# Key and query stacks made in place in 32-partition bands, with three banded score products per unit

## What is computed

```python
def gnn(h_target, h_neigh, adjacency, Wq, bq, Wk, bk, Wv, bv, Wo, bo, E):
    msg = h_neigh[None, :, :] + E[edge_types]          # edge_types is the adjacency
    q = (h_target @ Wq.T + bq).reshape(Bt, H, DH)      # h_target = layernorm(x)
    k = (msg @ Wk.T + bk).reshape(Bt, Bn, H, DH)
    v = (msg @ Wv.T + bv).reshape(Bt, Bn, H, DH)
    scores = jnp.einsum('bhd,bnhd->bhn', q, k) / np.sqrt(DH)
    scores = jnp.where(adjacency[:, None, :] == 0, -1e9, scores)
    attn = jnp.where(adjacency[:, None, :] == 0, 0.0, softmax(scores))
    return jnp.einsum('bhn,bnhd->bhd', attn, v).reshape(Bt, d) @ Wo.T + bo
x = x + gnn(...)
x = x + ffn(layernorm(x))   # tree: 8 levels, node = 2*node + (score > 0) + 1,
                            # out += gelu(|score|) * (x @ w2s[node] + b2s[node])
```

## Time and profile before

| what | us |
|---|---|
| median of three runs | 159.88 (159.72 to 160.49) |
| the profiled execution's own time | 160.56 |
| its span, first to last instruction | 157.9 |
| setup, to the first scores (L492 starts) | 23.6 |
| units 0 to 7 | 23.6 to 38 |
| units 8 to 31 | 38 to 76 |
| projection, tree walk, sorting | 76 to 107 |
| loop over the nodes | 107 to 158 |

### The profile page before, as it was taken

The page is one execution under the profiler, slowest core; times in us unless marked ns, Lnnn a source line. Parts: engine busy times, 40 slices in busy tenths (PEclk is TensorE's granted clock), DMA queues, the critical chain, the costliest instruction groups (busy, mean ns, idle before and its releaser), DMA issues.

```text
span 157.9 us, 3163 instructions
## 1 busy us (share of the span) xinstructions
PE 105.4 (67%) x870; PEld 78.5 (50%) x871; DVE 109.5 (69%) x302; ACT 73.5 (47%) x174; POOL 40.1 (25%) x82
## 2 busy tenths in 40 slices
...
GB/s 144 293 128 158 173 116 14 57 83 150 393 407 401 457 452 415 399 460 437 311 44 28 0 0 0 53 18 0 0 4 0 0 2 0 0 33 0 0 17 17
DMA packets 6341, 22.35 MB, mean 142 GB/s; under 512 B 1755, under 2 KB 4826, under 8 KB 5722
## 3 DMA queue, kind: packets, MB, share of 16 engines
...
q10 hardware_dynamic: 1104, 0.92, 2.0%
q0 software_dynamic: 256, 0.52, 1.1%
...
...
## 4 chain that ended last, share of the span: by engine, by line
PE 32%; DVE 19%; DMA 14%; issue 13%; ACT 8%; SPq 6%; POOL 3%; DVEq 3%; ACTq 0%; POOLq 0%
PE s_ps L660 10%; DMA early<-q_parts 7%; SPq L249 6%; PE turn_ps L523 4%; PE turn_ps L660 4%; ACT prob L391 4%; DVE prob L770 3%; DMA w_sb<-in_w_t 2%; PE aux_ps L660 2%; ACT prob_t L387 2%; POOL early L337 2%; DMA q_parts<-q_p 2%; PE misc_ps L660 2%; PE s_ps L492 2%; PE s_ps L502 2%
## 5 line engine op out<-in xcount | busy, mean ns | idle before, releaser
L523 PE MATMUL turn_ps<-ident,prob 128*128 128x128 f32 x128 | 23.0, 308 | 7.9 <-ACT prob L391 6.6
L391 ACT ACTIVATE prob<-prob,negmax 128x512 f32<-128x512 f32 x32 | 23.0, 720 | 9.6 <-DVE negmax L770 9.5
L349 POOL TENSOR_TENSOR early<-early,scaled_sb 128x128 f32<-128x128 f32 x48 | 20.5, 454 | 26.0 <-ACT scaled_sb L443 25.4
L777 DVE TENSOR_TENSOR prob_t<-turn_ps,prob_t 128x512 f16<-128x512 f32 x32 | 22.1, 689 | 6.2 <-ACT prob_t L387 6.2
L770 DVE CUSTOM_DVE_ANT_0 prob<-s_ps,mask 128x512 f32<-128x512 f32 x32 | 21.7, 682 | 6.5 <-PE s_ps L492 6.4
L660 PE MATMUL s_ps<-w,msg 128*128 x128 | 19.2, 295 | 7.9 <-issue 4.2
L523 PEld LDWEIGHTS turn_ps<-ident,prob 128*128 128x128 f32 x128 | 15.8, 155 | 16.3 <-ACT prob L391 15.5
L492 PE MATMUL s_ps<-early 96*128 96x512 bf16 x32 | 13.8, 437 | 13.2 <-DMA early<-q_parts 12.2
L660 PEld LDWEIGHTS s_ps<-w,msg 128*128 128x128 f32 x128 | 16.3, 200 | 10.4 <-issue 10.4
L387 ACT ACTIVATE prob_t<-turn_ps 128x512 f16<-128x512 f32 x32 | 18.6, 580 | 6.1 <-PE s_ps L502 5.6
L443 ACT ACTIVATE scaled_sb<-s_ps,coef 128x128 f32<-128x128 f32 x32 | 10.0, 363 | 20.8 <-PE s_ps L660 20.8
...
## 6 DMA issues: line engine op xcount, KB each, us to landing
...
w<-in_w_t SPq DMA_DIRECT2D x1, 4032.0 KB, 41.5
prob<-in_adj SPq DMA_DIRECT2D x1, 1024.0 KB, 9.8
...
msg<-in_neigh_t SPq DMA_DIRECT2D x1, 256.0 KB, 2.9
```

Source lines behind the costliest of these rows:

```text
L349: ins = nc.gpsimd.tensor_tensor(mine, mine, scaled_sb[:, i, :], ALU.add)
L391: nc.scalar.activation(prob[:, u % RING, :], prob[:, u % RING, :], ACT.Exp, bias=negmax[:, t, h:h + 1], scale=-1.0, accum_out=psums[:, t, ...
L523: last = nc.tensor.transpose(turn_ps[u % 2][:, m * P:(m + 1) * P], prob[:, u % RING, m * P:(m + 1) * P], ident[:])
L777: nc.vector.tensor_tensor(prob_t[:, v % 2, 1, :], turn_ps[v % 2][:], prob_t[:, v % 2, 0, :], ALU.subtract).then_inc(lo_moved, 1)
```

## The change

The weights' rows for keys and queries are laid out twice: in groups of four heads, each head having a band of 32 partitions in which each of its 16 channels stands twice (`twice`, `SIDE = 2`). A product with them makes the keys of four heads, every channel in two partitions, so `w_sb` grows from four to six blocks of 128 columns and two matmuls of each kind take the place of one.

A band then holds two parts of each channel, the even 16 partitions one and the odd 16 another. `mixed` (DVE) does that: result = part * side + whole, with side -1 in one kind of partition and 0 in the other, so that it gives the rest in one kind and the whole in the other. Three products over a band of 32 rows (`PRODUCTS`) give the six pairs of before. PE makes two units at a time: for each of the three products, one matmul of unit 2p and one of unit 2p+1, whose heads lie in neighbouring bands and whose results go to different banks. There are four score banks now, and the banks of the weighted values are `aux_ps` and `misc_ps`.

The DRAM round trips are gone, with `k_p`, `q_p` and `stack`. SP issues the `w2` loads as soon as the adjacency and `w1` have landed. The intermediate keys and queries (`k_f`, `k_r`, `k_0`, `k_1`, `q_f`, `q_r`) and the adjacency lie in the last quarter of `w2`, so its load waits until they have been used. Parts that the first units don't need (keys of heads 4 to 7, queries of tiles 1 to 3, masks of tiles 1 to 3, value parts) are made between units 0 to 7, by ACT, DVE and POOL. PE starts with 12 matmuls on zeros (`WARM_UP`). The loads of x and of the neighbours change places.

```diff
+SIDE = 2
+BANDS = 4
+BAND = P // BANDS
+PRODUCTS = ((0, 0), (0, 1), (1, 2))
...
-            sp.wait_ge(k_split, 2 * PARTS)
-            sp.dma_start(k_parts.rearrange("i p n -> p i n"), k_p[:]).then_inc(k_out, 16)
-            for i, (lo, hi) in enumerate(Q_SLICES):
-                sp.wait_ge(q_split[i], 2 * PARTS)
-                sp.dma_start(q_parts.rearrange("i p n -> p i n")[:, :, lo:hi], q_p[:, :, lo:hi]).then_inc(q_out[i], 16)
-                if i == 0:
-                    sp.wait_ge(k_out, 16)
-                    stack(sp, k_st, k_parts, K_RUNS, k_stacked)
-                sp.wait_ge(q_out[i], 16)
-                stack(sp, q_st, q_parts, Q_RUNS, q_stacked[i], lo, hi)
-            sp.wait_ge(k_stacked, 16 * len(K_RUNS))
             sp.wait_ge(b2_zero, 1)
             sp.dma_start(b2_sb[:, 0, :], b2[0:P, :]).then_inc(b2_in, 16)
             sp.dma_start(b2_sb[0:NODES - P, 1, :], b2[P:NODES, :]).then_inc(b2_in, 16)
+            sp.wait_ge(adj_in, 16)
+            sp.wait_ge(w1_in, 16)
             per = NODES_PAD // W2_PARTS
             for i in range(W2_PARTS):
                 n0, n1 = i * per, min((i + 1) * per, NODES)
+                if n0 == SPLIT_AT:
+                    sp.wait_ge(mask_ready, 2)
+                    for g in range(SIDE):
+                        sp.wait_ge(k_first[g], 2)
+                        sp.wait_ge(k_third[g], 1)
+                    for part in range(len(Q_SLICES)):
+                        sp.wait_ge(q_second[part], 1)
+                        sp.wait_ge(q_mixed[part], 1)
+                        sp.wait_ge(q_third[part], 1)
...
+            pool.wait_ge(q_first[1], 1)
+            nc.gpsimd.tensor_tensor(q_st[:, 1, :, P:], q_f[:, :, P:], q_st[:, 0, :, P:], ALU.subtract
+                                    ).then_inc(q_second[1], 1)
...
+            def keys(g):
+                act.wait_ge(k_done, g + 1)
+                nc.scalar.activation(k_0[:, g, :], score_ps[g], ACT.Identity, bias=col_sb[:, BK + g:BK + g + 1]
+                                     ).then_inc(k_moved[g], 1)
+                nc.scalar.activation(k_f[:, g, :], score_ps[g], ACT.Identity, bias=col_sb[:, BK + g:BK + g + 1]
+                                     ).then_inc(k_moved[g], 1)
+            def key_second(g):
+                act.wait_ge(k_first[g], 2)
+                nc.scalar.activation(k_1[:, g, :], k_r[:, g, :], ACT.Copy).then_inc(k_second[g], 1)
+            def query(i, g, bank):
+                lo, hi = Q_SLICES[i]
+                act.wait_ge(q_done[i], (SIDE, g + 1)[i])
+                nc.scalar.activation(q_f[:, g, lo:hi], bank, ACT.Identity, bias=bq_scaled[:, g:g + 1], scale=-SCALE
+                                     ).then_inc(q_moved[i], 1)
+            def query_first(i):
+                lo, hi = Q_SLICES[i]
+                act.wait_ge(q_moved[i], SIDE)
+                nc.scalar.activation(q_st[:, 0, :, lo:hi], q_f[:, :, lo:hi], ACT.Copy).then_inc(q_first[i], 1)
+            def value_part(i):
                 act.wait_ge(v_split, 2 * i + 1)
                 nc.scalar.activation(v_st[:, :, :, i, :].rearrange("p m h c -> p (m h) c"),
                                      v_f.rearrange("p (a c) -> p a c", c=DH), ACT.Copy).then_inc(v_split, 1)
+            act.wait_ge(col_in, 16)
+            keys(0)
+            act.wait_ge(bq_ready, 1)
+            for g in range(SIDE):
+                query(0, g, turn_ps[1][:, g * P:(g + 1) * P])
+            query_first(0)
+            key_second(0)
+            keys(1)
+            value_part(0)
...
+                if u == 0:
+                    value_part(1)
+                if u == 1:
+                    key_second(1)
+                if u == 2:
+                    query(1, 0, misc_ps[:, P:])
+                    value_part(2)
+                if u == 3:
+                    query(1, 1, misc_ps[:, P:])
+                    query_first(1)
...
+            pe.wait_ge(idle_ready, 1)
+            for _ in range(WARM_UP):
+                nc.tensor.matmul(score_ps[3], idle[:, 0:P], idle, start=True, stop=True)
             pe.wait_ge(msg_ready, 1)
-            nc.tensor.matmul(aux_ps[:], w_sb[:, 1, :], msg[:], start=True, stop=True).then_inc(k_done, 1)
-            for i, ((lo, hi), (t0, t1)) in enumerate(zip(Q_SLICES, TILE_SLICES)):
-                pe.wait_ge(h_ready, i + 1)
-                transposes(turn_ps[i], h_sb, h_turned, t0, t1)
-                if i == 1:
-                    for m in range(NT):
-                        last = nc.tensor.matmul(turn_ps[0][:, m * D:(m + 1) * D], msg[:, m * P:(m + 1) * P],
-                                                w_sb[:, 2, :], start=True, stop=True)
-                    last.then_inc(v_done, 1)
-                    pe.wait_ge(k_split, 1)
-                pe.wait_ge(ht_ready, i + 1)
-                nc.tensor.matmul((misc_ps, aux_ps)[i][:, 0:hi - lo], w_sb[:, 0, :], h_t[:, lo:hi],
-                                 start=True, stop=True).then_inc(q_done[i], 1)
-            def scores(u):
-                t, h = divmod(u, HEADS)
-                if u >= 2:
-                    pe.wait_ge(masked, u - 1)
-                if u == HEADS:
-                    pe.wait_ge(q_stacked[1], 16 * len(Q_RUNS))
-                nc.tensor.matmul(score_ps[u % 2], q_st[0:STACK, h, t * P:(t + 1) * P], k_st[0:STACK, h, :],
-                                 start=True, stop=True).then_inc(scored, 1)
+            nc.tensor.matmul(score_ps[0], w_sb[:, WK, :], msg[:], start=True, stop=True).then_inc(k_done, 1)
...
+                for i, (k, q) in enumerate(PRODUCTS):
+                    for u in units:
+                        t, h = divmod(u, HEADS)
+                        g, band = divmod(h, BANDS)
+                        rows = slice(band * BAND, (band + 1) * BAND)
+                        ins = nc.tensor.matmul(score_ps[u % RING], q_st[rows, q, g, t * P:(t + 1) * P],
+                                               k_st[rows, k, g, :], start=(i == 0), stop=(i == len(PRODUCTS) - 1))
+                        if i == len(PRODUCTS) - 1:
+                            ins.then_inc(scored, 1)
...
+                if u >= 2 and u % 2 == 0 and u + 2 < UNITS and u not in LATE:
+                    scores(u // 2 + 1)
...
+            def mixed(out, part, side, whole):
+                return nc.vector.scalar_tensor_tensor(out=out, in0=part, scalar=side[:, 0:1], in1=whole,
+                                                      op0=ALU.mult, op1=ALU.add)
...
+            def keys_first(g):
+                dve.wait_ge(k_moved[g], 2)
+                mixed(k_st[:, 0, g, :], k_0[:, g, :], from_odd, k_f[:, g, :]).then_inc(k_first[g], 1)
+                mixed(k_r[:, g, :], k_0[:, g, :], from_even, k_f[:, g, :]).then_inc(k_first[g], 1)
+            def keys_third(g):
+                dve.wait_ge(k_second[g], 1)
+                dve.wait_ge(k_first[g], 2)
+                mixed(k_st[:, 1, g, :], k_1[:, g, :], from_even, k_r[:, g, :]).then_inc(k_third[g], 1)
...
+            for i, (t0, t1) in enumerate(TILE_SLICES):
+                normalise(x_sb, 1 + i, t0, t1)
+            dve.wait_ge(sides_ready, 2)
+            turn_back(0, turn_ps[0][:, 0:P])
+            keys_first(0)
+            dve.wait_ge(q_first[0], 1)
+            nc.vector.tensor_tensor(q_st[:, 1, :, 0:P], q_f[:, :, 0:P], q_st[:, 0, :, 0:P], ALU.subtract
+                                    ).then_inc(q_second[0], 1)
+            query_mixed(0)
+            query_third(0)
+            keys_third(0)
+            dve.wait_ge(adj_in, 16)
+            masks(0)
...
+                if u == 1:
+                    keys_first(1)
+                if u == 2:
+                    turn_back(1, misc_ps[:, P:])
+                if u == 3:
+                    keys_third(1)
+                if u == 4:
+                    masks(1)
+                if u == 5:
+                    query_mixed(1)
+                if u == 7:
+                    query_third(1)
...
-    by_channel = np.arange(D).reshape(HEADS, DH).T.reshape(-1)
-    wq, wk = g["L0_gnn_Wq"][by_channel], g["L0_gnn_Wk"][by_channel]
-    bq, bk = g["L0_gnn_bq"][by_channel], g["L0_gnn_bk"][by_channel]
+    twice = np.repeat(np.arange(HEADS).reshape(HEADS, 1, 1) * DH + np.arange(DH), 2, axis=1).reshape(-1)
+    wq, wk = g["L0_gnn_Wq"][twice], g["L0_gnn_Wk"][twice]
+    bq, bk = (g[name][twice].reshape(SIDE, P) for name in ("L0_gnn_bq", "L0_gnn_bk"))
```

199 lines of the change are left out of this document (118 added, 81 removed).

## The result

| what | before, us | after, us | predicted, us |
|---|---|---|---|
| median (four runs each) | 159.8 | 153.45 (152.62 to 154.59) | 150.6 (147.8 to 155.0) |
| profiled execution, and its span | 160.56, 157.9 | 152.62, 150.8 | 151.3 |
| first scores start | 23.57 | 12.29 | 12.5 |
| first minimum | 24.32 | 13.43 | 13.5 |
| minimum of unit 8 | 38.63 | 31.86 | 29.9 |

The ratio is 0.960, with a 95% interval of 0.953 to 0.968. In five later rounds the same kernel has 0.956 (0.950 to 0.963). The change is faster by 4%, where 6% was forecast.

What follows compares the result with a forecast made beforehand. DRAM round trips bound the first 38 us, DVE and ACT the steady loop. 8.7 + 1.1 less 0.5 gives 9.3 off 160.56, so 151.3, or 150.6 against the median; own range 149.4 to 152.0, 8 in 10 147.8 to 155.0.

Steps and rivals of the forecast that it cites:

- The setup: Before the first minimum: scores start at 12.5 against 23.57, first minimum at 13.5 against 24.32, 10.8 us earlier.
- The products: Steady loop: 24 score products per eight units overlap at 0.115 us each, PE 9.7 of 11.1, so 0 cost.
- the rival with the drain: Score products one after the other, plus 0.15 us twice per pair for tiling-mode changes: 158.1 us; no chance of its own.
- one after the other: Steady loop: products don't overlap, 0.23 us each, eight units take 12.4 against 11.1; 154.5 us, chance 0.13.
- slower than before: Steady loop: changing the row band empties the array, 0.38 us a product; 165.3 us, chance 0.05.
- PE's clock: Between the minima of units 8 and 9: 1.1 us vanish with the wait, if PE holds its clock.
- The rival with PE at 1.2 GHz: Until the steady loop: key matmuls cost 1.0 more, units 0 to 8 1.4 more; 153.0 us, chance 0.16 with longer waits.
- What moved into units 0 to 7: First minimum to unit 8's: DVE 14.7 us plus 1.7 waiting, 16.4 against 14.3 before; unit 8 at 29.9, 8.7 earlier.
- The loads of w2: Started at about 12 instead of 34.3, beside everything: cost 0, ending near 53.
- The faster loop: Steady loop: with four banks DVE runs at its own 10.48 per eight units, 0.6 less; 148.8 us, chance 0.12.
- The part after the attention: After the loop: nothing the change touches is on the chain, so it lasts 82 us as before.
- The sum: 8.7 + 1.1 = 9.8, less 0.5 for hand-overs, gives 9.3: 151.3 us for the profiled execution, 150.6 for the median.

Runs made afterwards that it cites:

- the one-band kernel: Changed kernel with all score products reading partitions 0 to 31, whatever the head (times only): 180.79 us; six products take 1.46 us.
- with the clock held: Changed kernel plus 36 extra matmuls on zeros ahead of the first scores and 71 ahead of the transposes of units 0 to 9: 150.75 us, ratio 0.944.

## Why the prediction was right, and where it was off

The median of 153.45 is outside the forecast's own range (149.4 to 152.0). It is inside the wide one, which took in the lower clock.

**The setup** was right: 12.29 for 12.5 and 13.43 for 13.5. Each long step held: x at 3.92, the first key matmul to 7.4, the warm-up ending at 6.33 just ahead of what it covers. The mixes take 0.74 to 0.75 each, not 0.69, and some other steps less.

**The products** were right in the step that no row of before could show. I took 0.115 a product, and three steps of 0.216 us for six are 0.108 each. What I put at nothing is the change between 32 and 128 rows, 0.09 at each side of the six; with it a product costs 0.14, still under the 0.175 up to which the steady loop holds. In the rival with the drain I had priced it at 0.15, twice a pair; it is there at 0.09, and costs no time where PE has room. The rivals "one after the other" and "slower than before" fell with the one-band kernel, whose 1.46 shows what they would have been.

**The step that failed is PE's clock.** I credited 1.1 us that "vanish with the wait, if PE holds its clock", and took 2.4 GHz for units 0 to 11. In place of that stretch of 3 us came two, of 10 and of nearly 7. (The first units of before were at the lower level too, as I read from the earlier trace rows, but there the wait for the second stack took up what they lost.) The rival with PE at 1.2 GHz was the nearer one, in its time (153.0) and in one of its two reasons: it gave units 0 to 8 1.4 more, and from the first minimum to that of unit 8 they took 1.44 more (18.43 against 16.99 with the clock held). The other reason, 1.0 for slow key matmuls, was wrong, since the warm-up did its work. What it left out is the second stretch: units 8 to 11 take 1.07 more (5.35 against 4.28). That these two are equal, and 153.0 so near to 153.45, is luck. With 0.24 ahead of the first minimum (13.43 against 13.19) the lower clock makes 2.75, and the attention ends at 68.88 against 66.13. Even the credit was mis-sized: of 1.1, the clock was 0.5.

**What moved into units 0 to 7** was 0.6 too low. With the clock held the stage takes 16.99 us where I had 16.4:

```profile
13.19:30.18 16.99, 13.14 (x158) 9.24 (x159) 15.45 (x30) 12.66 (x28) 8.70 (x14) 1.00 0.96 414
```

DVE is busy 15.45 of it, for the 14.7 of my list, and waits 1.5 for 1.7. What the list had no price for is DVE beside POOL, which costs 0.95 at the first mix and 0.3 at a later one (1.41 against 1.08 for the same size). A first minimum 0.3 early hides half of the error, so unit 8 comes at 30.18 against 29.9. **The loads of w2** were right at 0, and the last, issued at 30.2, lands 22.8 later, at 53. **The faster loop** did not come: 11.10 for eight units, four banks or two. **The part after the attention** took 81.9. The 0.9 us by which the time outside the span shrank (2.7 to 1.8) isn't part of any step of mine; in the kernel of before this share was 1.7 to 3.0 over the runs, and I did not look for its cause.

**The sum**, on the profiled execution: 151.3, plus 2.4 at the end of the attention, less 0.1 behind it and 0.9 outside the span, gives the 152.6 measured, within rounding. The median lies 0.8 above that, as its executions differ in how long the clock is low.
